# Turning a tile of activations with VectorE block turns and block transfers in place of TensorE transposes

## The chip, the cores and the metric

The kernel runs on one core of a Trainium2 chip. The metric is the device time of one execution in microseconds (us). The engines are TensorE (PE in the profile; its weight loads are PEld), VectorE (DVE), ScalarE (ACT), GpSimd (POOL) and SyncE (SP, which here only issues DMA transfers). SBUF is the on-chip memory of 128 partitions, PSUM the eight banks that TensorE writes its products to, and HBM the memory outside.

## The reference

The input `x` is 2048 rows of 512. Each row is normalised, and two branches are added to it: an attention-like retrieval from a fixed memory, and a dense layer with int8 weights.

```python
xn = _layernorm(x, axis=-1)
# retrieval; only every 4th head of q is used, and each is repeated 4 times
q = (xn @ Wq.T + bq).reshape(b, s, 32, 128)
q_sel = (elu(q) + 1.0)[:, :, ::4, :]                      # 8 heads of 128
num = jnp.einsum('bshd,hde->bshe', q_sel, M)
den = jnp.einsum('bshd,hd->bsh', q_sel, z)[..., None] + 1e-6
out_heads = jnp.repeat(num / den, 4, axis=2)
attn = out_heads.reshape(b, s, 4096) @ Wo.T
# dense
ffn = jnp.einsum('bsd,df->bsf', xn, w.astype(jnp.float32) * w_scale) + b
return x + attn + ffn
```

The kernel multiplies M and Wo (summed over its 4 repeats) once into `P`, so that per row there are three products: q (512 to 1024), dense (512 to 512), and attn (1024 to 512), whose left side is `a` = (elu(q) + 1) / den.

## The kernel before

The rows are cut into 16 tiles (`t`) of 128. Every product is done in three passes of 32-bit matmuls, high times high, high times low and low times high, for which each operand is split into a part rounded to `float32r` (`_hi`, by ScalarE) and a rest (`_lo`, by VectorE). Weights, `WqT`, `wd` and `P`, are split once; `xT` and `aT`, the transposed activations, once a tile.

What each engine does, and in which order, is written out by hand. A list of about 40 lines a engine covers the loading and splitting of weights, the products q, dense of tiles 0 to 6 and the eight products that make `P` (`product_P`). From tile 7 (`LEAD`) a loop over `t` runs, and after tile 15 a tail, since the attention product stands 7 tiles behind q. In one turn `t` of the loop:

- TensorE does `product_q(t)` in two halves, `product_dense(t)`, the spreading of a mean (`spread_mean`), `product_attn(t - 7)` and `transpose_a(t - 5)`; in the tail only `product_attn` and `transpose_a`.
- VectorE adds the bias (`add_bias`), makes `s` = elu(q) + 1 (`make_s`) in a ring of 7 buffers, sums `s` times z over each head (`denominator`), splits `aT_lo` (`split_aT_lo`) and adds the finished products to `x` (`add_dense`, `add_attn`).
- ScalarE does the exponential, divides `s` by its head's denominator in place (`make_a`, eight activations a tile), and copies `aT` to `aT_hi` (`copy_aT_hi`).
- GpSimd multiplies `s` by z (`times_z`), adds `b`, centres `xT`.
- SP issues the loads of `x` and `xT` and the stores of the finished tiles.

`transpose_a` is 8 matmuls of 128x128 against a unit matrix `ident`. They turn `a` of a tile, rows on partitions, into `aT`, columns on partitions, in the two PSUM banks `aT_ps`; `copy_aT_hi` and `split_aT_lo` read them there. The buffers `aT_hi` and `aT_lo` have two places, so a copy for tile t waits until `product_attn(t - 2)` is done (`attn_filled`).

Of the kernel before, what the change touches and what calls it, by code (L numbers as in the profile page):

```python
# [15 lines left out]
DEN_EPS = 1e-6  # L16


def retrieval_and_dense(nc, x_d, xT_d, WqT_d, bq_d, WoT_d, MT_d, z_d, w_d, wscale_d, b_d, out_d):
# [4 lines left out]
    G, D = z_d.shape  # L24
# [7 lines left out]
    SRING = 7  # L32
    XRING = 4
    HRING = 4
    BEHIND = 4
    assert P == D and HID == 512 and HALF == 512 and R == 4 and T == 16 and G == 8 and K == 4

    with ExitStack() as ctx:
# [35 lines left out]
        den = sb("den", [P, G])  # L74
        den_e = sb("den_e", [P, G])
        rden = sb("rden", [P, 2, G])
        warm_b = sb("warm_b", [P, HID], BF16)

        warm_r = P_hi[:, 0, :]
        w_i8 = w_words[:].bitcast(I8)  # L80
        WqT_raw = sbuf_s[:, 0:K, :]
        wd_raw = sbuf_s[:, K:K + 2, :].rearrange("p r (a n) -> p (r a) n", n=HID)
        ebuf = e_and_sz[:, 0, :]
        szbuf = e_and_sz[:, 1, :]
        w_f32 = e_and_sz[:].rearrange("p r (a n) -> p (r a) n", n=HID)
# [8 lines left out]
        def q_bank(t, h):  # L94
            return ([q_ps, attn_ps, aT_ps][t % 3] if t < LEAD else q_ps)[h]
# [13 lines left out]
        consts_set = sem("consts_set")  # L109
        stats_set = sem("stats_set")  # L110
# [27 lines left out]
        den_e_ready = sem("den_e_ready")  # L138
# [5 lines left out]
        aT_filled = sem("aT_filled")  # L144
# [15 lines left out]
        def _(sp):  # L160
# [24 lines left out]
            sp.dma_start(w_words[:], w_d).then_inc(w_in, 16)  # L185
# [9 lines left out]
            sp.dma_start(z_b[:].rearrange("p (g d) -> p g d", g=G),  # L195
                         z_d.unsqueeze(0).to_broadcast([P, G, D])).then_inc(z_in, 16)
            sp.dma_start(b_b[:], b_d.unsqueeze(0).to_broadcast([P, HID])).then_inc(b_in, 16)
            for t in range(5, T):
                if t >= FIRST_LENT:
                    sp.wait_ge(P_filled, t - FIRST_LENT + 1)  # L200
                load_x(t)
                load_xT(t)
                if t >= 10:
                    sp.wait_ge(attn_added, t - 9)
                    sp.dma_start(out_d[t - 10], x[:, t - 10, :]).then_inc(stored, 16)
            for t in range(T - 10, T - 1):
                sp.wait_ge(attn_added, t + 1)
                sp.dma_start(out_d[t], x[:, t, :]).then_inc(stored, 16)
# [7 lines left out]
        def _(pool):  # L216
# [31 lines left out]
            def times_z(t, h):  # L248
                if t == 0 and h == 0:
                    pool.wait_ge(z_in, 16)  # L250
                if t == 0:
                    pool.wait_ge(wd_by_pool, 1)
# [3 lines left out]
                nc.gpsimd.tensor_tensor(szbuf[:, halves(h)], sbuf_s[:, t % SRING, halves(h)],  # L256
                                        z_b[:, halves(h)], ALU.mult).then_inc(sz_ready, 1)
# [20 lines left out]
            scale_w()  # L278
            rstd_of(3)
# [20 lines left out]
            center(7)  # L300
            add_b(0)
# [9 lines left out]
            for t in range(T - BEHIND, T):  # L311
                times_z(t, 0)
                times_z(t, 1)
                add_b(t - BEHIND + 2)
            for t in range(T - 2, T):
                add_b(t)

        @block.scalar
        def _(act):
# [58 lines left out]
            def copy_aT_hi(t):  # L378
                for h in range(2):
                    act.wait_ge(aT_filled, 2 * t + h + 1)  # L380
                    if t >= 2:
                        act.wait_ge(attn_filled, t - 1)
                    nc.scalar.activation(aT_hi[:, t % 2, h * GH:(h + 1) * GH, :].rearrange("p g r -> p (g r)"),  # L383
# [514 lines left out]
```

## Time and profile before

| | |
|---|---|
| median of 3 runs | 260.02 us (259.87 to 264.77) |
| the profiled execution | 260.27 us |
| its span, from the first to the last instruction | 258.5 us |
| TensorE busy | 249.9 us, 97% of the span |
| VectorE, ScalarE, GpSimd busy | 156.2, 121.2, 103.2 us |
| bytes moved by DMA | 26.42 MB, mean 102 GB/s |
| TensorE's granted clock | 1.0 in all 40 slices |

The profile comes from one execution, whose own time is 1.8 us above its span and 0.25 us above the median of the runs. Busy time is added up per engine and engines run beside each other, so a share near 100% names the engine to look at first, and the chain of waits tells whether it sets the end. Ends of matmuls are modelled: they overlap, and the pitch from start to start is what one costs.

### The profile page before, as it was taken

The numbers are of one execution on the slowest core, as the hardware profiler recorded it, in microseconds if no ns is written. First come the engines' busy times: TensorE is split into PE (matmuls) and PEld (weight loads), VectorE is DVE, ScalarE is ACT, GpSimd is POOL, SyncE is SP. The second block draws the span as 40 slices with busy tenths as digits, with TensorE's granted clock in tenths as the row PEclk, the third lists the DMA queues.
The fourth block names the chain that finished last, engine by engine and source line by source line (L and its number), as shares of the span: only waits on it lengthen the run. The fifth ranks groups of instructions, "written<-read, shape, count | busy, mean of one in ns | idle before, by whom it ended". The sixth has DMA issues, their size and how long they took to land.

```text
span 258.5 us, 3387 instructions
## 1 busy us (share of the span) xinstructions
PE 249.9 (97%) x1156; PEld 201.2 (78%) x1156; DVE 156.2 (60%) x262; ACT 121.2 (47%) x276; POOL 103.2 (40%) x96
## 2 busy tenths in 40 slices
PE   6899899899998999999999999999999999999996
PEld 4477687687766888888888888888888888888885
DVE  4849996898677846457483746557463445555321
ACT  3653625657457554444345553544345345555100
POOL 2594745580303670705235070714305055563000
PEclk9999999999999999999999999999999999999999
DMA  7999999995400003030302103010101001111111
GB/s 247 414 411 406 345 228 218 209 217 153 146 16 4 0 13 109 0 124 1 122 1 66 58 0 122 3 41 0 41 3 41 1 1 43 41 41 43 49 49 64
DMA packets 9808, 26.42 MB, mean 102 GB/s; under 512 B 1088, under 2 KB 1344, under 8 KB 8640
## 3 DMA queue, kind: packets, MB, share of 16 engines
q1 hardware_dynamic: 8640, 19.40, 20.2%
q0 software_dynamic: 864, 6.29, 11.8%
q10 hardware_dynamic: 288, 0.52, 0.6%
q8 instruction: 9, 0.15, 0.2%
q14 instruction: 7, 0.06, 0.1%
HBM read 22.02 MB, written 4.19 MB: 101 GB/s over the span
## 4 chain that ended last, share of the span: by engine, by line
PE 84%; DVE 9%; ACT 2%; issue 2%; DMA 1%; DVEq 0%
PE attn_ps L679 11%; PE attn_ps L677 11%; PE attn_ps L678 11%; PE q_ps L677 8%; PE q_ps L679 8%; PE q_ps L678 8%; PE aT_ps L752 5%; PE dense_ps L677 5%; PE dense_ps L678 5%; PE dense_ps L679 5%; PE attn_ps L740 2%; DMA x<-in_x 1%; DVE stats L462 1%; DVE wd_lo L517 1%; DVE q_ps L531 1%
## 5 line engine op out<-in xcount | busy, mean ns | idle before, releaser
L256 POOL TENSOR_TENSOR e_and_sz<-s,z_b 128x512 f32<-128x512 f32 x32 | 41.7, 1330 | 31.4 <-DVE den L543 31.4
L375 ACT ACTIVATE s<-s,rden 128x128 f32<-128x128 f32 x128 | 39.2, 389 | 31.0 <-DVE rden L550 31.0
L677 PE MATMUL attn_ps<-P_hi,aT_hi 128*128 128x512 f32 (+1 forms) x128 | 50.2, 393 | 0.0
L679 PE MATMUL attn_ps<-P_hi,aT_lo 128*128 128x512 f32 (+1 forms) x128 | 49.2, 385 | 0.0
L678 PE MATMUL attn_ps<-P_lo,aT_hi 128*128 128x512 f32 (+1 forms) x128 | 49.0, 382 | 0.0
L570 DVE TENSOR_TENSOR x<-attn_ps,x 128x512 f32<-128x512 f32 x15 | 10.4, 691 | 46.4 <-PE attn_ps L679 46.4
L677 PE MATMUL q_ps<-WqT_hi,xT_hi 128*128 128x512 f32 x88 | 36.0, 409 | 0.6 <-DVE s L538 0.6
L679 PE MATMUL q_ps<-WqT_hi,xT_lo 128*128 128x512 f32 x88 | 34.4, 391 | 0.0
L678 PE MATMUL q_ps<-WqT_lo,xT_hi 128*128 128x512 f32 x88 | 34.3, 390 | 0.0
L219 POOL TENSOR_TENSOR rstd<-vareps,neg_half 128x1 f32<-128x1 f32 x16 | 10.6, 665 | 55.7 <-DVE vareps L470 55.7
L225 POOL TENSOR_TENSOR xT<-xT,mean_b 128x512 f32<-128x512 f32 x14 | 19.6, 1403 | 32.5 <-ACT mean_b L324 32.5
L531 DVE SCALAR_TENSOR_TENSOR q_ps<-q_ps,rstd,bq_b 128x512 f32<-128x512 f32 x24 | 18.1, 758 | 21.5 <-PE q_ps L679 21.5
L362 ACT ACTIVATE e_and_sz<-q_ps 128x512 f32<-128x512 f32 x24 | 14.3, 596 | 33.9 <-DVE q_ps L531 33.9
L679 PEld LDWEIGHTS attn_ps<-P_hi,aT_lo 128*128 128x128 f32 x128 | 24.1, 188 | 4.9
L677 PEld LDWEIGHTS attn_ps<-P_hi,aT_hi 128*128 128x128 f32 x128 | 24.1, 188 | 4.9
L678 PEld LDWEIGHTS attn_ps<-P_lo,aT_hi 128*128 128x128 f32 x128 | 24.1, 188 | 4.4
L677 PE MATMUL dense_ps<-wd_hi,xT_hi 128*128 128x512 f32 x64 | 25.6, 400 | 1.2 <-DVE x L554 1.2
L383 ACT ACTIVATE aT_hi<-aT_ps 128x512 fp32r<-128x512 f32 x32 | 17.4, 595 | 17.0 <-PE aT_ps L752 17.0
L679 PE MATMUL dense_ps<-wd_hi,xT_lo 128*128 128x512 f32 x64 | 24.9, 390 | 0.0
L678 PE MATMUL dense_ps<-wd_lo,xT_hi 128*128 128x512 f32 x64 | 24.9, 390 | 0.0
L563 DVE TENSOR_TENSOR aT_lo<-aT_ps,aT_hi 128x512 fp32r<-128x512 f32 x32 | 20.6, 685 | 5.2 <-ACT aT_hi L383 5.2
L364 ACT ACTIVATE e_and_sz<-e_and_sz 128x512 f32<-128x512 f32 x32 | 20.2, 632 | 1.0
(93 smaller groups left out, 407.9 us busy)
## 6 DMA issues: line engine op xcount, KB each, us to landing
x<-in_WoT POOLq DMA_DIRECT2D x6, 1024.0 KB, 9.6
x<-in_x SPq DMA_DIRECT2D x16, 256.0 KB, 3.7
xT<-in_xT SPq DMA_DIRECT2D x16, 256.0 KB, 4.1
out<-x SPq DMA_DIRECT2D x15, 256.0 KB, 2.0
x<-in_WoT SPq DMA_DIRECT2D x2, 1024.0 KB, 14.6
s<-in_WqT SPq DMA_DIRECT2D x3, 512.0 KB, 7.0
s<-in_w_scale SPq DMA_DIRECT2D x1, 1024.0 KB, 10.1
s<-in_WqT ACTq DMA_DIRECT2D x2, 256.0 KB, 4.2
```

The source lines that it names most:

```text
L225: nc.gpsimd.tensor_tensor(xT[:, t % XRING, :, :], xT[:, t % XRING, :, :], mean_b[:, t % 2, :].unsqueeze(1).to_broadcast([P, K, P]), ALU.su ...
L256: nc.gpsimd.tensor_tensor(szbuf[:, halves(h)], sbuf_s[:, t % SRING, halves(h)], z_b[:, halves(h)], ALU.mult).then_inc(sz_ready, 1)
L362: nc.scalar.activation(e, q_bank(t, h)[:], ACT.Relu, scale=-1.0).then_inc(qneg_ready, 1)
L364: nc.scalar.activation(e, e, ACT.Exp, scale=-1.0).then_inc(exp_ready, 1)
L375: last = nc.scalar.activation(a_g, a_g, ACT.Copy, scale=rden[:, t % 2, g:g + 1])
L383: nc.scalar.activation(aT_hi[:, t % 2, h * GH:(h + 1) * GH, :].rearrange("p g r -> p (g r)"), aT_ps[h][:], ACT.Copy).then_inc(aT_hi_ready, 1)
L531: nc.vector.scalar_tensor_tensor(q_bank(t, h)[:], q_bank(t, h)[:], rstd[:, t:t + 1], bq_b[:, halves(h)], ALU.mult, ALU.add).then_inc(q_bia ...
L563: nc.vector.tensor_tensor(aT_lo[:, t % 2, gs, :].rearrange("p g r -> p (g r)"), aT_ps[h][:], aT_hi[:, t % 2, gs, :].rearrange("p g r -> p ...
L677: nc.tensor.matmul(out, x_hi, w_hi, start=start, stop=False)
L678: nc.tensor.matmul(out, x_hi, w_lo, start=False, stop=False)
L679: return nc.tensor.matmul(out, x_lo, w_hi, start=False, stop=stop)
L752: last = nc.tensor.transpose(aT_ps[h][:, i * P:(i + 1) * P], sbuf_s[:, t % SRING, g * D:(g + 1) * D], ident[:])
```

## The change

The transposes leave TensorE. A 128x128 transpose is made of 32x32 blocks that are turned inside a quarter of the partitions, and a move of each block from its quarter of the partitions to another.

- `turn_blocks(t)`: one VectorE instruction turns all 32x32 blocks of `s` of a tile (128x1024) in place.
- `spread_blocks(t)`: SP issues 16 transfers a tile, SBUF to SBUF, each of 32 partitions by 256 elements (1 KB runs), from partition quarter i and column quarter j to partition quarter j and place i of `aT`. Tiles take two places in turn: a new buffer `aT` and the buffer of `MT`, which is free once `P` is made.
- For that q, bq, z and `s` are laid out by quarters of heads (first columns 0 to 31 of all 8 heads, then 32 to 63, and so on). `make_a` and `times_z` now read and write rows of 32 elements (`by_quarter`), and `copy_aT_hi` and `split_aT_lo` read SBUF in place of PSUM (`by_head`, `in_groups`).
- The epsilon of the denominator becomes a 129th column of each head's products, which the sum takes along; the instruction that added it goes.
- The two PSUM banks of `aT` become two more banks of q, so that q of a tile has to wait for `s` of the tile before the last one only.
- `make_a` and the sums run one tile earlier (`BEHIND` 3 for 4), the ring of `s` has 6 places for 7. SP's list is written anew around the 16 transfers. The matmuls that keep TensorE at work at the start read a 128x128 bf16 tile, 8 and 6 of them for 7 and 5, and two early loads change places.

```diff
-    SRING = 7
+    SRING = 6
-    BEHIND = 4
+    BEHIND = 3
...
-        q_ps = [bank("q0_ps"), bank("q1_ps")]
-        aT_ps = [bank("aT0_ps"), bank("aT1_ps")]
+        q_ps = [bank(f"q{i}_ps") for i in range(4)]
...
+        def by_quarter(v):
+            return v.rearrange("p (j g c) -> p j g c", g=G, c=D // 4)
+        def aT_place(t):
+            return [aT[:], MT[:].rearrange("p g d -> p (g d)").rearrange("p (i e) -> p i e", i=4)][t % 2]
+        def by_head(t, gs):
+            return aT_place(t).rearrange("p i (g r) -> p g i r", g=G)[:, gs]
...
+            def spread_blocks(t):
+                sp.wait_ge(a_turned, t + 1)
+                if t == 1:
+                    sp.wait_ge(P_filled, G)
+                elif t >= 2:
+                    sp.wait_ge(aT_lo_ready, 2 * t - 2)
+                for i in range(4):
+                    for j in range(4):
+                        sp.dma_start(aT_place(t)[j * 32:(j + 1) * 32, i, :],
+                                     sbuf_s[i * 32:(i + 1) * 32, t % SRING, j * E // 4:(j + 1) * E // 4]
+                                     ).then_inc(aT_in[t % 2], 16)
...
+            for t in range(LEAD, T):
+                if t + 4 < T:
+                    sp.wait_ge(P_filled, t + 4 - FIRST_LENT + 1)
+                    load_x(t + 4)
+                    load_xT(t + 4)
+                spread_blocks(t - BEHIND - 1)
+                if t - LEAD >= 1:
+                    store(t - LEAD - 1)
+            for t in range(T - BEHIND - 1, T):
+                spread_blocks(t)
+                store(t - BEHIND - 1)
...
             def copy_aT_hi(t):
+                act.wait_ge(aT_in[t % 2], aT_landed(t))
+                if t >= 2:
+                    act.wait_ge(attn_filled, t - 1)
...
-                nc.vector.reduce_sum(den[:], szbuf.rearrange("p (g d) -> p g d", g=G), AX.X
-                                     ).then_inc(den_ready, 1)
+                nc.vector.reduce_sum(den[:, t % 2, :], sz_eps, AX.X).then_inc(den_ready, 1)
                 dve.wait_ge(den_ready, t + 1)
-                nc.vector.tensor_scalar_add(den_e[:], den[:], DEN_EPS).then_inc(den_e_ready, 1)
...
+            def turn_blocks(t):
+                dve.wait_ge(a_ready, t + 1)
+                nc.vector.transpose(sbuf_s[:, t % SRING, :], sbuf_s[:, t % SRING, :]).then_inc(a_turned, 1)
...
-            def transpose_a(t):
-                pe.wait_ge(a_ready, t + 1)
...
-                transpose_a(t - LEAD + 2)
```

On TensorE, at the end of a turn of the loop, the order before is this; L679 is the last pass of `product_attn`, L752 `transpose_a`, and L677 the first pass of the next `product_q`.

```order
637 L677 MATMUL attn_ps<-P_hi,aT_hi 128x512
638 L678 MATMUL attn_ps<-P_lo,aT_hi 128x512
639 L679 MATMUL attn_ps<-P_hi,aT_lo 128x512
640 L752 MATMUL aT_ps<-ident,s 128x128 x8
641 L677 MATMUL q_ps<-WqT_hi,xT_hi 128x512
642 L678 MATMUL q_ps<-WqT_lo,xT_hi 128x512
```

The same place now has no row between the last pass of `product_attn` and `product_q`.

On SP, from the last loads to the end of the program, the order before:

```order
46 L162 DMA x<-in_x 128x512 [waits P_filled]
47 L167 DMA xT<-in_xT 128x512 [waits xT_lo_ready]
48 L205 DMA out<-x 128x512 [waits attn_added]
49 L208 DMA out<-x 128x512 [waits attn_added] x9
50 L212 DMA out<-x 128x256 [waits attn_added] x2
51 L38 UNCONDITIONAL_BRANCH [waits stored]
```

And after the change, from the blocks of tile 12 to the end; L200 is `spread_blocks`, L206 `store`.

```order
75 L200 DMA aT<-s 32x256 [waits aT_lo_ready,a_turned]
76 L200 DMA aT<-s 32x256 x15
77 L206 DMA out<-x 128x512 [waits attn_added]
78 L200 DMA MT<-s 32x256 [waits aT_lo_ready,a_turned]
79 L200 DMA MT<-s 32x256 x15
80 L206 DMA out<-x 128x512 [waits attn_added]
81 L200 DMA aT<-s 32x256 [waits aT_lo_ready,a_turned]
82 L200 DMA aT<-s 32x256 x15
83 L206 DMA out<-x 128x512 [waits attn_added]
84 L200 DMA MT<-s 32x256 [waits aT_lo_ready,a_turned]
85 L200 DMA MT<-s 32x256 x15
86 L206 DMA out<-x 128x512 [waits attn_added] x4
```

Sixteen transfers of tiles 12, 13, 14 and 15 each now stand in SP's queue in the tail, with a store of an earlier tile between them; before there were only stores.

On VectorE, from the last `add_dense` of the loop into the tail, the order before:

```order
207 L554 SCALAR_TENSOR_TENSOR x<-dense_ps,rstd,x 128x512
208 L543 TENSOR_REDUCE den<-e_and_sz 128x8
209 L546 TENSOR_SCALAR den_e<-den 128x8
210 L550 RECIPROCAL rden<-den_e 128x8
211 L570 TENSOR_TENSOR x<-attn_ps,x 128x512
212 L563 TENSOR_TENSOR aT_lo<-aT_ps,aT_hi 128x512 x2
```

And after the change:

```order
209 L599 SCALAR_TENSOR_TENSOR x<-dense_ps,rstd,x 128x512
210 L591 TENSOR_REDUCE den<-e_and_sz 128x8
211 L595 RECIPROCAL rden<-den 128x8
212 L591 TENSOR_REDUCE den<-e_and_sz 128x8
213 L595 RECIPROCAL rden<-den 128x8
214 L619 TENSOR_TENSOR x<-attn_ps,x 128x512
215 L612 TENSOR_TENSOR aT_lo<-aT,aT_hi 128x512 x2
216 L604 STREAM_TRANSPOSE s<-s 128x1024
```

Two sums, of tiles 12 and 13, stand there in a row now, and the turn of tile 12 stands behind `add_attn(8)` and `split_aT_lo(10)`.

## Rows read from the trace of the kernel before

**Rows 1.** The page: busy time by engine (us, share, instructions), and the chain by engine.

```profile
PE 249.9 (97%) x1156; PEld 201.2 (78%) x1156; DVE 156.2 (60%) x262; ACT 121.2 (47%) x276; POOL 103.2 (40%) x96
...
PE 84%; DVE 9%; ACT 2%; issue 2%; DMA 1%; DVEq 0%
```

**Rows 2.** Busy time in four stretches: end of P, loop, tail, last tile.

```profile
core 0: us, PE busy (x) PEld busy (x) DVE busy (x) ACT busy (x) POOL busy (x), PEclk, DMA share, GB/s
74.88:81.27 6.39, 5.70 (x27) 3.27 (x26) 5.46 (x10) 4.91 (x13) 0.33 (x1) 1.00 0.00 0
81.27:211.89 130.62, 130.62 (x612) 108.21 (x611) 73.96 (x128) 60.85 (x144) 51.78 (x46) 1.00 0.11 37
211.89:249.50 37.61, 37.61 (x191) 31.68 (x190) 17.88 (x30) 16.34 (x44) 14.36 (x12) 1.00 0.11 43
```

**Rows 3.** The chain in order of time: start us, us, what; transposes alone.

```profile
109.73 0.87 PE aT_ps L752 x8
...
124.38 0.87 PE aT_ps L752 x8
...
237.45 0.87 PE aT_ps L752 x8
...
243.82 0.87 PE aT_ps L752 x8
```

**Rows 4.** Timeline of PE at the end of `P`, before tile 7.

```profile
79.19 1.10 PE L740 MATMUL attn_ps<-x,MT 128*128 128x512 f32 x2 [0.69 <-DVE P_lo L522]
80.13 1.04 PE L752 MATMUL aT_ps<-ident,s 128*128 128x128 f32 x8
81.00 0.27 PE L687 MATMUL mean_ps<-ident,meanvar 128*128 128x128 f32 x1
```

**Rows 5.** Timeline of DVE there.

```profile
80.49 0.18 DVE L466 BATCH_NORM_AGGREGATE meanvar<-stats 128x2 f32<-128x6 f32 x1
```

**Rows 6.** Timeline of SP's queue: loads issued one behind another, and lone stores.

```profile
1.65 0.42 SPq L162 DMA_DIRECT2D x<-in_x  x1
2.12 0.43 SPq L170 DMA_DIRECT2D s<-in_WqT  x1
...
15.60 2.34 SPq L162 DMA_DIRECT2D x<-in_x  x1
...
250.90 0.33 SPq L208 DMA_DIRECT2D out<-x  x1
```

**Rows 7.** DMA queue of SP and ACT (packets, MB, share of 16 engines), and stores to landing.

```profile
q1 hardware_dynamic: 8640, 19.40, 20.2%
...
out<-x SPq DMA_DIRECT2D x15, 256.0 KB, 2.0
```

**Rows 8.** Timeline of DVE in the last turn of the loop.

```profile
203.93 0.76 DVE L531 SCALAR_TENSOR_TENSOR q_ps<-q_ps,rstd,bq_b 128x512 f32<-128x512 f32 x1 [1.88 <-PE q_ps L679]
...
206.01 0.69 DVE L538 SCALAR_TENSOR_TENSOR s<-q_ps,e_and_sz 128x512 f32<-128x512 f32 x1 [0.74 <-ACT e_and_sz L364]
...
207.31 1.21 DVE L543 TENSOR_REDUCE den<-e_and_sz 128x8 f32<-128x1024 f32 x1
```

**Rows 9.** Timeline of POOL and of PE (first pass of `product_attn(8)`) there.

```profile
208.60 2.54 POOL L256 TENSOR_TENSOR e_and_sz<-s,z_b 128x512 f32<-128x512 f32 x2 [10.71 <-DVE den L543]
...
206.44 0.39 PE L677 MATMUL attn_ps<-P_hi,aT_hi 128*128 128x512 f32 x1
```

**Rows 10.** Timeline of DVE and ACT behind `product_attn(8)`.

```profile
212.09 0.69 DVE L570 TENSOR_TENSOR x<-attn_ps,x 128x512 f32<-128x512 f32 x1 [2.90 <-PE attn_ps L679]
213.16 1.29 DVE L563 TENSOR_TENSOR aT_lo<-aT_ps,aT_hi 128x512 fp32r<-128x512 f32 x2 [0.38 <-ACT aT_hi L383]
...
212.53 1.09 ACT L383 ACTIVATE aT_hi<-aT_ps 128x512 fp32r<-128x512 f32 x2 [0.85 <-PE aT_ps L752]
```

**Rows 11.** Timeline of DVE and POOL at 18 to 21 us.

```profile
18.70 2.53 DVE L500 TENSOR_TENSOR xT_lo<-xT,xT_hi 128x512 fp32r<-128x512 f32 x1 [3.77 <-ACT xT_hi L339]
...
18.29 2.39 POOL L237 TENSOR_TENSOR s<-e_and_sz,s 128x1024 f32<-128x1024 f32 x1 [0.43 <-ACT e_and_sz L349]
```

More of the change, by code:

```diff
@@ L94, in q_bank @@
         def q_bank(t, h):
-            return ([q_ps, attn_ps, aT_ps][t % 3] if t < LEAD else q_ps)[h]
+            if t < LEAD and t % 3 == 1:
+                return attn_ps[h]
+            return q_ps[2 * (t % 3 == 2 if t < LEAD else t % 2) + h]
         def last_attn_ps(c):
@@ L143, in retrieval_and_dense @@
         dense_added = sem("dense_added")
-        aT_filled = sem("aT_filled")
+        a_turned = sem("a_turned")
+        aT_in = [sem(f"aT_in{i}") for i in range(2)]
         aT_hi_ready = sem("aT_hi_ready")
@@ L194, in _ @@
             load_xT(4)
-            sp.dma_start(z_b[:].rearrange("p (g d) -> p g d", g=G),
-                         z_d.unsqueeze(0).to_broadcast([P, G, D])).then_inc(z_in, 16)
+            sp.dma_start(z_b[:], z_d.unsqueeze(0).to_broadcast([P, E])).then_inc(z_in, 16)
             sp.dma_start(b_b[:], b_d.unsqueeze(0).to_broadcast([P, HID])).then_inc(b_in, 16)
-            for t in range(5, T):
-                if t >= FIRST_LENT:
-                    sp.wait_ge(P_filled, t - FIRST_LENT + 1)
+            for t in range(5, FIRST_LENT):
                 load_x(t)
                 load_xT(t)
[L203 to L208, printed above, removed]
+            spread_blocks(0)
+            for t in range(FIRST_LENT, LEAD + 4):
+                sp.wait_ge(P_filled, t - FIRST_LENT + 1)
+                load_x(t)
+                load_xT(t)
+            spread_blocks(1)
+            spread_blocks(2)
+            for t in range(LEAD, T):
[9 more added lines that the diff above has]
+                store(t - BEHIND - 1)
+            for t in range(T - BEHIND - 1, T - 1):
+                store(t)
             for c in range(2):
@@ L300, in _ @@
             center(7)
+            times_z(3, 0)
+            times_z(3, 1)
             add_b(0)
@@ L313, in _ @@
                 times_z(t, 1)
-                add_b(t - BEHIND + 2)
-            for t in range(T - 2, T):
+                add_b(t - 3)
+            for t in range(T - 3, T):
                 add_b(t)
@@ L441, in _ @@
             copy_mean(8)
+            make_a(3)
             for t in range(LEAD, T):
-                copy_aT_hi(t - LEAD + 1)
                 exp_of(t, 0)
@@ L452, in _ @@
                 copy_aT_hi(t)
-                if t + 2 < T:
-                    make_a(t + 2)
+                if t + BEHIND < T:
+                    make_a(t + BEHIND)
         @block.vector
@@ L633, in _ @@
             split_P_lo(1)
+            turn_blocks(1)
             add_dense(5)
@@ L648, in _ @@
             split_P_lo(7)
+            turn_blocks(2)
             for t in range(LEAD, T):
-                split_aT_lo(t - LEAD + 1)
                 add_bias(t, 0)
@@ L658, in _ @@
                 make_s(t, 1)
+                split_aT_lo(t - LEAD + 1)
                 add_dense(t)
                 denominator(t - BEHIND)
+                if t == T - 1:
+                    denominator(T - BEHIND)
                 add_attn(t - LEAD)
@@ L741, in product_P @@
                                  ).then_inc(P_filled, 1)
-            def transpose_a(t):
-                pe.wait_ge(a_ready, t + 1)
-                for h in range(2):
-                    if t == 0:
-                        pe.wait_ge(s_ready, 11 + h)
-                    else:
-                        pe.wait_ge(aT_lo_ready, 2 * t - 1 + h)
-                    for i in range(GH):
-                        g = h * GH + i
-                        last = nc.tensor.transpose(aT_ps[h][:, i * P:(i + 1) * P],
-                                                   sbuf_s[:, t % SRING, g * D:(g + 1) * D], ident[:])
-                    last.then_inc(aT_filled, 1)
             def product_attn(t):
@@ L765, in product_attn, with keep_busy @@
                 last.then_inc(attn_filled, 1)
[L767 to L771 removed]
+            def keep_busy(n):
+                for i in range(n):
+                    nc.tensor.matmul(dense_ps[:], warm[:], warm[:].unsqueeze(1).to_broadcast([P, 4, P]), start=True, stop=True)
+            pe.wait_ge(warm_set, 1)
+            keep_busy(8)
             pe.wait_ge(consts_set, 3)
             spread_mean(0)
[L774 to L775 removed]
+            keep_busy(6)
             hi_hi(0, 0, 0)
```

98 lines of the change are left out of this document (48 added, 50 removed).

## The prediction

> **What bounds the kernel now.** I read the page's busy times first, then the chain of waits, then the busy time by stretch, and last the timelines of single engines. TensorE is busy 97% of the span, and 84% of the chain that ended last is its own work [rows 1]. The stretches show where that is strictly so: from tile 7 to the end of the loop it is busy 130.62 of 130.62 us, and in the tail 37.61 of 37.61 [rows 2]. VectorE, ScalarE and GpSimd stand at 74, 61 and 52 us in the loop's 131. So whatever leaves TensorE's list there comes off the end, as long as nobody else is late. The transposes of one tile cost 0.87 us on the chain, whichever tile; they come every 14.65 us in the loop (109.73 to 124.38) and every 6.37 us in the tail (237.45 to 243.82) [rows 3]. Without them a turn of the loop would be 13.78 us. A `product_attn` is 5.45 us (from 206.44 to 211.89, where the third stretch of the windows begins) [rows 2, 9], which is also what a tile of the tail would cost.
>
> **Part 1, the transposes go.** Sixteen tiles are turned: nine in the loop (tiles 2 to 10), five in the tail (11 to 15), two before tile 7. In loop and tail nothing else stands between TensorE's products, so 14 x 0.87 = 12.2 us go. The two before tile 7 save nothing: there the products of `P` wait for their own split (0.69 us before the last one at 79.19), a wait that takes in what the first transpose gives up, and `spread_mean(8)` needs a mean that VectorE has at 80.49 + 0.18 = 80.67, against TensorE's 81.00 now [rows 4, 5]. That leaves 0.3 us, and the new turn and sum on VectorE in that stage (about 2.6 us, partly in its waits) may cost as much or a little more: I take 0, with -0.5 to +0.9 as bounds of the gain. The span without new waits is 258.5 - 12.2 = 246.3 us.
>
> **Part 2, VectorE.** It gets one turn of 128x1024 a tile and loses one small addition. No row shows a turn; the nearest is the sum over 128x1024, 1.21 us [rows 8], which I take; the upper bound is GpSimd's 2.39 us for the same size [rows 11]. `split_aT_lo` now has two SBUF operands. Such an instruction took 2.53 us at 18.70 while GpSimd's ran from 18.29 for 2.39, so it waited for it to end [rows 11]; the split from PSUM took 1.29 for two [rows 10]. That is up to 1.3 us a half more. The loop's cover holds: 73.96 us busy in nine turns is 8.2 a turn, and 8.2 + 1.2 + 2.6 = 12.0 is below 13.78. Cost in the loop 0; with the cover gone each us above it would cost nine. The Trainium skill (VectorE: DVE Perf Modes, section "The three transpose paths", and its rules for authors) speaks against this trade: it gives 390 ns for a 128x128 bf16 transpose on TensorE and 311 on VectorE, in blocks only, and says to use TensorE where PSUM will do. By its figure eight of them are 2.5 us of VectorE, which the loop would still cover; the rows price TensorE's eight at 0.87 us, less than a third of its figure.
>
> **Part 3, ScalarE and GpSimd.** `make_a` and `times_z` get rows of 32 elements for 128 or 512; sizes stay. I take the same durations, and twice as the bound. ScalarE has 60.85 us busy in nine turns, 6.8 of 13.78, GpSimd 5.8 [rows 2]; doubling these parts still fits. Cost 0. The new q banks loosen a wait that TensorE does not have in this stretch: 0. The start keeps its order but for two loads: 0, give or take 0.3.
>
> **Part 4, SP's queue.** Sixteen transfers a tile are issued one behind another by one engine. SP's loads at the start are issued every 0.47 us (1.65, 2.12), 0.42 to 0.43 us long; a lone store after a wait takes 0.33 [rows 6]. All these have 128 rows; a transfer of 32 rows is in no row. If the price is one of the instruction and not of its rows, it is 0.47 us; if rows count, it goes towards the 0.33 of the lone one plus the gap of 0.04, or 0.37. I take 0.47, since 4 KB rows (2.12) are issued as fast as 2 KB rows (1.65), and a lone instruction may have been made ready during its wait. In the loop 16 x 0.47 + 3 x 0.47 = 8.9 us a turn fit in 13.78, and each tile's blocks have two turns of time: cost 0. In the tail a tile lasts 5.45 us and SP needs 16 x 0.47 + 0.47 = 8.0. There it decides.
>
> **The tail, step by step.** Let T be the end of `product_attn(8)`, 211.89 in the trace before. What is worked out here is relative to it, so the gain of part 1 shifts all alike. VectorE's last turn: `add_bias` at 203.93, 0.66 to its next instruction, turn(11) 1.2, two `make_s` 1.3, the two splits of tile 9 1.3, `add_dense` 0.6 (make_s and it lie 1.30 apart from 206.01 to 207.31), sum and reciprocal of tile 12 1.5: 210.5 [rows 8]. The sum of tile 13 needs two `times_z`, 2.54 us [rows 9], begun when the first sum is over: 212.9, its own 1.4 to 214.3. Then `add_attn(8)` 0.7, the splits of tile 10 1.3, the turn of tile 12 1.2 [rows 10]: 217.5, or T + 5.6. GpSimd works on tile 14 just then, so I add 0.6 for one wait of a split: T + 6.2, bounds T + 5.6 and, with a turn of 2.4 and two full waits, T + 9. Now SP issues tiles 12 to 15: 64 transfers and 3 stores between them, 67 x 0.47 = 31.5. The last lands 2.0 us after its issue begins [rows 7], which adds 1.5, and then half a copy to `aT_hi` and half a split, 1.3 [rows 10], stand before `product_attn(15)`: T + 6.2 + 31.5 + 1.5 + 1.3 = T + 40.5. TensorE could begin it at T + 6 x 5.45 = T + 32.7. It is 7.8 us late, shared as waits before tiles 13 (about 2.6), 14 and 15. With pitch p the lateness is 7.8 - 66 x (0.47 - p).
>
> **Sum.** 246.3 + 7.8 = 254.1 us span; the profiled execution lies 1.8 above its span, and the median 0.25 below that: 255.6 us.
>
> **The rivals.**
>
> *The small transfers are issued faster.* At 0.37 us the tail is late by 7.8 - 6.6 = 1.2 us: 249.0 us. With all bounds in its favour it is 247.5, at 0.42 it is 252.3. For it: the lone store, 0.33 us, and a quarter of the rows. Against it: no issue in a series, whatever its bytes, was below 0.42. The Trainium skill (DMA: Bandwidth & Descriptors, section "Issuing engines are not separate DMA queues") is on this side: it calls the issuing time usually small beside the transfer. The rows of SP show 0.47 us an issue beside 2.0 us to landing for 256 KB, and a block has 32 KB.
>
> *The transfers themselves hold the queue back.* When the queue was full in the first 20 us, one issue took 2.34 us [rows 6]. A block is 32 packets of data and, by the 144 packets of a 128-row load (8640 for 60 transfers), 16 more: 3 an engine. Packets took 20.2% of 16 x 258.5 us for 8640, 97 ns each [rows 7], so a block would need 0.29 us, under the pitch. If a packet within SBUF took 0.2 us, the pitch were 0.6 and the tail 8.6 us later: 264.2. This is the case on the other side. From 0.54 on it is no gain at all, from 0.62 slower by over 2%, and above 0.77 the loop's 13.78 us are exceeded too.
>
> *The strided operands cost double, or the turn.* VectorE's tail then starts SP two to three us later, and a few waits enter the loop: 257 to 260 us.
>
> *The change does not do what it says:* were aT not ready early in the loop (tile 1 waits for all of `P`), TensorE would wait at tile 8 or 9. SP has from 80 us on 7.5 us an issue of a tile, and `product_attn(1)` comes 22 us later, so I give this no time of its own.
>
> **How the numbers follow.** The forecast, a pitch between 0.43 and 0.50 (253 to 257.5), 0.45. Faster issue, 247 to 253, 0.37. Held back by transfers, 258 to 272, 0.11. Strides, 0.07. The predicted time is 255.6 us. The range of 8 in 10 leaves out the lowest of the fast case and the upper part of the held-back one: 247.5 to 261. Within 2% (254.8 to 265.2) is about what a measurement of this kernel can tell from no change; the forecast lies just inside. Faster by over 2%: all of the fast case and some 0.13 of the forecast, 0.50. Slower by over 2%: 0.06. Between: 0.44.
>
> **What would show it.** Part 1: no transposes on PE, turns of the loop 13.8 us apart, PE busy all of it. Part 4: SP's issues of 32x256 every 0.47 us in runs of 16, no gap between runs from tile 12 on; PE idle before `product_attn(13)`, (14) and (15) for about 2.6 us each, released by VectorE's `aT_lo`, that by ScalarE's `aT_hi`, that by DMA. If PE is idle in the loop, a cover of part 2 or 3 has failed; if the tail has no idle PE, the pitch was lower. I would be most wrong if the transfers queue up.

## The result

The changed kernel takes 270.86 us (median of 4, 269.67 to 271.33) where the kernel before takes 260.0: the ratio is 1.041, with a 95% interval from 1.037 to 1.046. It is slower by 4%; I had forecast 255.6 us and given a slower kernel 6 in 100. Runs of the kernel before spread from 259.8 to 264.9 us, for a reason that no run here shows, so every experiment below has its ratio to runs of that kernel on the same chip, and two experiments are compared by their own times and by their profiled spans.

The page of the changed kernel, first the busy times, then the granted clock in 40 slices, SP's queue, the chain by engine and by line, and the costliest group:

```profile
PE 245.0 (91%) x1030; PEld 191.5 (71%) x1030; DVE 176.4 (65%) x261; ACT 119.8 (44%) x276; POOL 106.0 (39%) x97
...
PEclk9999999999999999999999999999999999868968
...
q1 hardware_dynamic: 20928, 27.81, 31.8%
...
PE 61%; SPq 18%; DVE 10%; issue 4%; ACT 3%; DMA 2%; DVEq 0%
SPq L200 18%; PE q_ps L734 9%; PE q_ps L736 9%; PE q_ps L735 8%; PE attn_ps L734 7%; PE attn_ps L736 7%; PE attn_ps L735 7%; PE dense_ps L734 4%; PE dense_ps L736 4%; PE dense_ps L735 4%; PE attn_ps L797 2%; DVE stats L510 1%; DMA x<-in_x 1%; DVE wd_lo L565 1%; DVE s L586 1%
...
L734 PE MATMUL attn_ps<-P_hi,aT_hi 128*128 128x512 f32 (+1 forms) x128 | 53.4, 417 | 14.8 <-DVE aT_lo L612 14.8
```

TensorE's share of the chain fell from 84% [rows 1] to 61%, and one line of SP's queue, the issue of the sixteen transfers, holds 18% of the span. TensorE waits 14.8 us for `aT_lo` in all. Where that is, the busy times by stretch say (loop, tail in four pieces, the product of tile 13 alone, and the first 6 us of the last product):

```profile
core 0: us, PE busy (x) PEld busy (x) DVE busy (x) ACT busy (x) POOL busy (x), PEclk, DMA share, GB/s
...
100.00:206.00 106.00, 106.00 (x466) 86.51 (x465) 75.09 (x110) 52.65 (x128) 42.27 (x38) 1.00 0.29 86
...
220.00:230.00 10.00, 7.23 (x31) 5.56 (x30) 3.03 (x4) 3.49 (x10) 1.35 (x2) 1.00 0.26 75
230.00:240.00 10.00, 5.03 (x13) 3.67 (x12) 3.02 (x4) 1.15 (x2) 0.00 (x0) 0.67 0.26 75
240.00:250.00 10.00, 7.22 (x25) 5.54 (x24) 1.90 (x3) 1.15 (x2) 0.00 (x0) 0.84 0.24 71
250.00:260.00 10.00, 5.72 (x24) 4.61 (x24) 1.90 (x3) 1.15 (x2) 0.00 (x0) 0.84 0.34 112
...
234.00:240.00 6.00, 4.39 (x10) 3.48 (x11) 3.02 (x4) 1.15 (x2) 0.00 (x0) 0.50 0.30 89
...
258.00:264.00 6.00, 6.00 (x28) 6.00 (x29) 1.56 (x3) 0.00 (x0) 0.00 (x0) 0.50 0.20 74
```

The loop is full, as it was before [rows 2]: the cover of VectorE, ScalarE and GpSimd held. The tail, full before, is not: TensorE has 7.23, 5.03, 7.22 and 5.72 us of work in four times 10 us, and its granted clock falls, to half (1.2 GHz) while it works on tile 13 and again in the last product. VectorE, ScalarE and GpSimd idle too, so none of them is the bound. SP's queue is what never rests:

```profile
201.31 10.01 SPq L200 DMA_DIRECT2D MT<-s  x16
211.35 0.58 SPq L206 DMA_DIRECT2D out<-x  x1
212.03 10.02 SPq L200 DMA_DIRECT2D aT<-s  x16
222.09 0.58 SPq L206 DMA_DIRECT2D out<-x  x1
222.77 10.03 SPq L200 DMA_DIRECT2D MT<-s  x16
...
233.52 10.01 SPq L200 DMA_DIRECT2D aT<-s  x16
...
244.25 11.02 SPq L200 DMA_DIRECT2D MT<-s  x16
```

Sixteen issues take 10.0 us, and a tile 10.74 (212.03 to 222.77), so an issue costs 0.633 us with its gap, where I had taken 0.47. A tile of the tail needs 5.60 us of TensorE (5.45 before the change). The chain in order of time shows the same issues one by one, and then the steps by which the last tile reaches TensorE:

```profile
247.34 1.60 SPq L200
...
254.05 0.59 SPq L200
254.69 1.87 DMA MT<-s
256.58 0.64 ACT aT_hi L431
257.24 0.70 DVE aT_lo L612
257.99 0.58 PE attn_ps L734
```

The last transfer lands 1.87 us after its issue began, and issues follow one another every 0.63 us (254.05, 254.69): the transfers themselves are quick, the issues are what queues. By the shares of the queue in the two profile pages (31.8% of 16 x 269.4 us, less 20.2% of 16 x 258.5) the 12288 packets of the blocks took some 44 ns each, an estimate, so 48 of them on 16 engines take 0.13 us. TensorE's waits in the tail, in the brackets of its timeline, are before the products of tiles 12 to 15:

```profile
224.81 0.47 PE L734 MATMUL attn_ps<-P_hi,aT_hi 128*128 128x512 f32 x1 [2.77 <-DVE aT_lo L612]
235.61 0.77 PE L734 MATMUL attn_ps<-P_hi,aT_hi 128*128 128x512 f32 x1 [4.97 <-DVE aT_lo L612]
246.35 0.47 PE L734 MATMUL attn_ps<-P_hi,aT_hi 128*128 128x512 f32 x1 [2.78 <-DVE aT_lo L612]
257.99 0.58 PE L734 MATMUL attn_ps<-P_hi,aT_hi 128*128 128x256 f32 x1 [4.28 <-DVE aT_lo L612]
```

The matmul at 235.61 takes 0.77 us and the one at 246.35 takes 0.47: the first runs at the lower clock, as do the matmuls behind it up to 240 us. The releaser named is VectorE, but VectorE is idle there; followed back, it waits for ScalarE's copy, that for the landing, and that for the issue. This is the wait that the prediction describes, only larger, and it begins one tile earlier, before tile 12.

### The profile page after: what moved, and what is told of

It is laid out like the page before. It is cut to its first block, busy times and chain, and to the rows that moved or that the text cites. A ratio compares the mean times of both kernels' runs of the same rounds, so it can differ in the third digit from the quotient of the medians.

```text
span 269.4 us, 3377 instructions
## 1 busy us (share of the span) xinstructions
PE 245.0 (91%) x1030; PEld 191.5 (71%) x1030; DVE 176.4 (65%) x261; ACT 119.8 (44%) x276; POOL 106.0 (39%) x97
## 2 busy tenths in 40 slices
DMA packets 22097, 34.83 MB, mean 129 GB/s; under 512 B 5184, under 2 KB 13632, under 8 KB 20928
## 3 DMA queue, kind: packets, MB, share of 16 engines
q1 hardware_dynamic: 20928, 27.81, 31.8%
q0 software_dynamic: 864, 6.29, 11.4%
## 4 chain that ended last, share of the span: by engine, by line
PE 61%; SPq 18%; DVE 10%; issue 4%; ACT 3%; DMA 2%; DVEq 0%
SPq L200 18%; PE q_ps L734 9%; PE q_ps L736 9%; PE q_ps L735 8%; PE attn_ps L734 7%; PE attn_ps L736 7%; PE attn_ps L735 7%; PE dense_ps L734 4%; PE dense_ps L736 4%; PE dense_ps L735 4%; PE attn_ps L797 2%; DVE stats L510 1%; DMA x<-in_x 1%; DVE wd_lo L565 1%; DVE s L586 1%
## 5 line engine op out<-in xcount | busy, mean ns | idle before, releaser
L734 PE MATMUL attn_ps<-P_hi,aT_hi 128*128 128x512 f32 (+1 forms) x128 | 53.4, 417 | 14.8 <-DVE aT_lo L612 14.8
L298 POOL TENSOR_TENSOR e_and_sz<-s,z_b 128x512 f32<-128x512 f32 x32 | 42.8, 1367 | 43.1 <-DVE den L591 43.0
L735 PE MATMUL attn_ps<-P_lo,aT_hi 128*128 128x512 f32 (+1 forms) x128 | 52.2, 408 | 0.0
L734 PE MATMUL q_ps<-WqT_hi,xT_hi 128*128 128x512 f32 x104 | 41.8, 402 | 0.9 <-DVE s L586 0.6
L736 PE MATMUL q_ps<-WqT_hi,xT_lo 128*128 128x512 f32 x104 | 40.6, 390 | 0.0
L735 PE MATMUL q_ps<-WqT_lo,xT_hi 128*128 128x512 f32 x104 | 40.5, 390 | 0.0
L612 DVE TENSOR_TENSOR aT_lo<-MT,aT_hi 128x512 fp32r<-128x512 f32 x16 | 15.3, 993 | 17.6 <-ACT aT_hi L431 17.6
L586 DVE SCALAR_TENSOR_TENSOR s<-q_ps,e_and_sz 128x512 f32<-128x512 f32 x28 | 18.8, 676 | 7.9 <-DMA MT<-s 4.0
L734 PEld LDWEIGHTS q_ps<-WqT_hi,xT_hi 128*128 128x128 f32 x104 | 19.5, 188 | 6.0 <-issue 1.2
L612 DVE TENSOR_TENSOR aT_lo<-aT,aT_hi 128x512 fp32r<-128x512 f32 x16 | 14.8, 966 | 12.2 <-ACT aT_hi L431 12.2
L735 PEld LDWEIGHTS q_ps<-WqT_lo,xT_hi 128*128 128x128 f32 x104 | 19.5, 188 | 4.4 <-issue 0.5
```

The lines of the kernel that those rows point to most:

```text
L298: nc.gpsimd.tensor_tensor(sz_eps[:, :, h * D // 2:(h + 1) * D // 2].rearrange("p g (j c) -> p j g c", j=2), by_quarter(sbuf_s[:, t % SRING ...
L586: nc.vector.scalar_tensor_tensor(sbuf_s[:, t % SRING, halves(h)], q_bank(t, h)[:], 0.0, ebuf[:, halves(h)], ALU.max, ALU.add).then_inc(s_r ...
L612: nc.vector.tensor_tensor(in_groups(aT_lo[:, t % 2, gs, :]), by_head(t, gs), in_groups(aT_hi[:, t % 2, gs, :]).bitcast(F32), ALU.subtract) ...
L734: nc.tensor.matmul(out, x_hi, w_hi, start=start, stop=False)
L735: nc.tensor.matmul(out, x_hi, w_lo, start=False, stop=False)
L736: return nc.tensor.matmul(out, x_lo, w_hi, start=False, stop=stop)
```

## The experiments

Two questions stood: is it the number of issues that costs, and what sets the price of one? And what makes up the rest, since 66 issues at 0.633 us explain some 11 of the 15 us by which the forecast was missed?

**Four issues for sixteen.** A transfer takes 32 rows with four runs each and writes all 128 partitions; the rows and columns of `a` come in another order, and the matrix `M` is laid out to fit.

```diff
-                    for j in range(4):
-                        sp.dma_start(aT_place(t)[j * 32:(j + 1) * 32, i, :],
-                                     sbuf_s[i * 32:(i + 1) * 32, t % SRING, j * E // 4:(j + 1) * E // 4]
+                    sp.dma_start(aT_place(t)[:, i, :],
+                                 sbuf_s[i * 32:(i + 1) * 32, t % SRING, :].rearrange("r (j c) -> r j c", j=4)
...
```

> The changed kernel with 4 transfers a tile in place of 16: each takes one quarter of the partitions (32 rows of 4 runs of 1 KB) and lays its runs on all 128 partitions in the order row, column quarter; M's columns are laid out to match, so the bytes moved and the result stay the same. Theory, a transfer has a price per instruction on SP of about 0.63 us whatever its rows: SP needs 4 x 0.63 + 0.6 = 3.1 us a tile, less than the 5.6 of a tile of the tail, so no product of the tail waits; the end of the eighth attention product at 205.0 us + 6 x 5.6 + 8.5 gives a span of 247 us and a time near 249 us. Rival, the price goes by runs or bytes: 4 issues take as long as 16 did, 10 us a tile, and the time stays near 270 us.

Measured: 248.81 us (248.55 to 249.08), ratio 0.947 (0.942 to 0.952). SP's queue and the tail by stretch:

```profile
211.74 2.50 SPq L199 DMA_DIRECT2D aT<-s  x4
214.28 0.59 SPq L205 DMA_DIRECT2D out<-x  x1
217.64 2.50 SPq L199 DMA_DIRECT2D MT<-s  x4
...
204.00:238.00 34.00, 34.00 (x148) 27.36 (x147) 24.64 (x28) 15.95 (x43) 16.58 (x12) 1.00 0.45 125
```

Each issue now moves four times the bytes and costs the same 0.63 us; SP waits between tiles, TensorE is full. The bytes are the same as with sixteen, 27.8 MB on this queue. The packets are fewer, 17856 for 20928, but took more of the engines' time together (36.1% of 16 x 247.1 us for 31.8% of 16 x 269.4), so the loss lay in the count of issues. With **eight** issues of 64 partitions a tile:

> The changed kernel with 8 transfers a tile, each of 32 rows of 2 runs laid on 64 partitions, M's columns laid out to match; bytes and result are the same. Theory, an issue within SBUF costs 0.60 us of SP (0.63 from start to start) whatever it carries: SP needs 8 x 0.63 + 0.63 = 5.7 us a tile in the tail, where TensorE needs 5.6, so the tail waits for a few tenths at most and the time is within 1 us of the kernel with 4, 248.8 us. Rival, halving the transfers halves the loss: about 259 us.

Measured: 249.13 us (248.44 to 249.66), ratio 0.954 (0.947 to 0.961), no wait of TensorE in the tail. Eight at 0.63 and a store are 5.7 us, level with the 5.6 us between two tiles. So up to eight issues the count costs nothing that the time shows; between eight and sixteen no run stands.

**What an issue costs.** Behind the end of the kernel before, seven batches of transfers are issued by SP, each batch waited for. They differ in rows, bytes, runs and in where the data lies.

```diff
+            for i in range(16):
+                sp.dma_start(sbuf_s[i % 4 * 32:(i % 4 + 1) * 32, 0, i // 4 * 256:(i // 4 + 1) * 256],
+                             sbuf_s[i // 4 * 32:(i // 4 + 1) * 32, 1, i % 4 * 256:(i % 4 + 1) * 256]
+                             ).then_inc(priced[0], 16)
+            sp.wait_ge(priced[0], 256)
...
+                sp.dma_start(sbuf_s[i % 4 * 32:(i % 4 + 1) * 32, 0, i // 4 * 256:(i // 4 + 1) * 256],
+                             x_d[i][i // 4 * 32:(i // 4 + 1) * 32, 0:256]).then_inc(priced[2], 16)
```

> The kernel before the change, and behind its last store seven batches on SP's queue, each waited for before the next: 16 transfers within SBUF of 32x256 between quarters, 16 within SBUF of 128x256, 16 from HBM of 32x256, 12 from HBM of 128x512, 16 within SBUF from 32 rows of 4 runs to 128x256, 16 within SBUF of 128x16 (64-byte runs), and 16 to HBM of 32x256. The issue durations of each are read from the trace. Theory, per instruction: the first, third and last batch come out at one duration and all lie within 0.42 to 0.63 us. Rival A, transfers within SBUF are dearer to issue than those that touch HBM: first, second, fifth and sixth near 0.6, the others near 0.43. Rival B, a slice of 32 partitions is dearer: first, third and last near 0.6, the others near 0.43.

SP's queue, in this order: within SBUF 32 rows of 1 KB; 128 rows of 1 KB; HBM to SBUF 32 rows of 1 KB; 128 rows of 2 KB (twelve of them); within SBUF 32 rows of four runs; 128 rows of 64 bytes; SBUF to HBM 32 rows of 1 KB:

```profile
259.27 10.11 SPq L217 DMA_DIRECT2D s<-s  x16
270.64 10.46 SPq L220 DMA_DIRECT2D s<-s  x16
282.60 7.31 SPq L223 DMA_DIRECT2D s<-in_x  x16
291.18 5.75 SPq L226 DMA_DIRECT2D s<-in_x  x12
302.18 10.40 SPq L229 DMA_DIRECT2D s<-s  x16
314.61 10.17 SPq L232 DMA_DIRECT2D s<-s  x16
325.99 7.29 SPq L235 DMA_DIRECT2D scratch<-s  x16
```

Divided by their counts: 0.63, 0.65, 0.46, 0.48, 0.65, 0.64, 0.46 us. Neither a quarter of the rows nor a sixteenth of the bytes changes it by more than 0.02 us; source and destination do. With HBM on one side an issue costs 0.46 to 0.48 us, with SBUF on both 0.63 to 0.65. A page of the Trainium skill (DMA: Bandwidth & Descriptors, section "Issuing engines are not separate DMA queues") calls the issuing time usually small beside the transfer. Here it is a third of the 1.8 us to landing, and since sixteen transfers overlap and their issues don't, it is the bound.

These are prices in a series of one kind. Part of the price stands with the neighbour: in the loop of the changed kernel a load from HBM takes 0.58 us directly behind the transfers within SBUF, and the load behind it 0.44.

```profile
112.36 0.58 SPq L178 DMA_DIRECT2D x<-in_x  x1
112.98 0.44 SPq L183 DMA_DIRECT2D xT<-in_xT  x1
```

The stores between two tiles of the tail take 0.58 us for the same reason, as far as these rows tell; what SP waits for there no run shows.

**Two queues.** In the tail (tiles 12 to 15) half of the sixteen are issued by ScalarE.

```diff
+                if t + 2 >= 12 and t + 2 < T:
+                    act.wait_ge(a_turned, t + 3)
+                    act.wait_ge(aT_lo_ready, 2 * (t + 2) - 2)
+                    for i in range(2, 4):
+                        for j in range(4):
+                            act.dma_start(aT_place(t + 2)[j * 32:(j + 1) * 32, i, :],
...
```

> The changed kernel, 16 transfers a tile, but those of tiles 12 to 15 issued half by SP and half by ScalarE's queue, there behind the copy of the tile two before and the scaling of the tile one after. Theory, each issuing engine pays for its own issues and the generators do not hinder each other: SP needs 5.7 us a tile, ScalarE 8 x 0.63 + 1.2 + 2.5 = 8.7, and the last tile lands some 13 us earlier than at 256.6: a span near 256 us and a time near 258. Rival, the issues of both share one generator: 10 us a tile again, and the time stays at 268 to 271 us.

Measured: 262.06 us (260.9 to 263.59), ratio 1.002 (0.997 to 1.007). From the timelines of ScalarE and of SP's queue:

```profile
238.38 5.30 ACTq L508 DMA_DIRECT2D MT<-s  x8
243.78 1.15 ACT L431 ACTIVATE aT_hi<-aT 128x512 fp32r<-128x512 f32 x2 [7.39 <-issue]
...
238.37 4.96 SPq L200 DMA_DIRECT2D MT<-s  x8
```

SP and ScalarE issue eight each at the same time, at 0.62 and 0.66 us an issue. So the price is paid per issuing engine, not in something that they share: some 9 us come back (262.06 for 270.86). That it is 4 us more than I expected (3.4 in the span, 259.4 for 256) is mostly my own edit: ScalarE's issues for tile 15 stand ahead of its copy for tile 14, which so begins at 243.78, and the product of tile 14 at 245.28, behind a wait of TensorE of 2.70 us.

**The clock.** Matmuls on unused data fill TensorE's waits in the tail (10, 20, 20 and 20 of them behind tiles 11 to 14).

```diff
+                if t >= T - LEAD + 2:
+                    keep_busy(10 if t == T - LEAD + 2 else 20)
```

> The changed kernel with 10, 20, 20 and 20 further bf16 matmuls of 128x512 on TensorE, of zeros into a PSUM bank that nobody reads any more, behind the attention products of tiles 11 to 14, where TensorE waits. Theory, the fall of the granted clock in the tail costs only what the last product takes longer, 8.7 us against about 5.9 at full clock: the granted clock stays at 1.0 for the last product, and the time falls by 2 to 3 us, to about 268 us. Rival, the waits alone make the loss: no difference, or up to 2 us more where the added matmuls overrun the gap.

Measured: 268.28 us (267.98 to 269.27), ratio 1.022 (1.016 to 1.028); its slowest run is below the fastest of the changed kernel (269.67), and the medians are 2.6 us apart. The granted clock stays at full where it was 0.67 and 0.84, and only the last product has no issue behind which to hide: it starts at 258.17 (257.99 in the changed kernel) and the span ends 8.6 us later where it was 11.4:

```profile
230.00:240.00 10.00, 8.21 (x37) 4.71 (x37) 3.02 (x4) 1.15 (x2) 0.00 (x0) 1.00 0.25 72
...
258.17 0.39 PE L734 MATMUL attn_ps<-P_hi,aT_hi 128*128 128x256 f32 x1 [0.46 <-DVE aT_lo L612]
```

So the clock costs 2.8 us of the span, all of it in the last product, a loss on top of the waits that go before it.

**The distance of two passes.** In the changed kernel the 24 passes of a product with `a` lie further apart than those of the other products. The first pass of `product_attn(8)` and the first of `product_attn(9)`, 24 places later, in the changed kernel:

```profile
199.48 0.39 PE L734 MATMUL attn_ps<-P_hi,aT_hi 128*128 128x512 f32 x1
...
205.08 0.40 PE L734 MATMUL attn_ps<-P_hi,aT_hi 128*128 128x512 f32 x1
```

That is 5.60 us for 24 places, 0.2333 each, where the other products have 0.227. The change put a buffer of 8224 bytes (`e_and_sz`, with the column for epsilon) ahead of `aT_hi`, which so lies 32 bytes off. A first try put 32 unused bytes behind it, so that `aT_hi` lies 64 bytes off:

> The changed kernel with 8 unused columns (32 bytes) behind the buffer of the exponentials and products with z, so that the buffers behind it, aT_hi and aT_lo first, start at a multiple of 64 bytes as before the change. Theory, the attention passes are issued every 0.233 us for 0.227 before, and their weight loads take 204 ns for 188, because aT_hi and aT_lo lie 32 bytes off: weight loads back to 188 ns, passes every 0.227 us, the eighth attention product ends 1.3 us earlier, and since SP's issues set the tail, the time falls by about 1.3 us only. Rival, the slower passes come from the block transfers that write SBUF beside them: weight loads stay at 204 ns, no difference.

Measured: 269.56 us (267.91 to 270.89), ratio 1.025 (1.019 to 1.031), and the passes still 0.2333 us apart. The profiled span is 269.3 us, as the changed kernel's 269.4, so I don't count the median as a gain. The expectation's 204 ns for a weight load was the mean of the whole trace of the changed kernel, the tail at half clock with it: from 100 to 200 us its loads take 188 ns, as before the change. The second try, on the kernel with four issues, allocates `e_and_sz` last, and `aT_hi` lies at a multiple of 2048 bytes:

```diff
-        e_and_sz = sb("e_and_sz", [P, E + G * (D + 1)])
...
         warm = sb("warm", [P, P], BF16)
+        e_and_sz = sb("e_and_sz", [P, E + G * (D + 1)])
```

> The kernel with 4 transfers a tile, and the buffer of the exponentials and products with z placed behind all other buffers in SBUF, so that aT_hi and aT_lo start at a multiple of 2048 bytes again, as before the change (in the changed kernel they lie 32 bytes off, and 64 in the kernel of the second experiment). Theory, the attention passes, 0.2333 us apart in every changed kernel so far at full clock against 0.227 before, are slower because of that address: they come back to 0.227, 24 x 0.006 x 16 = 2.3 us off the span of 247.1: 244.8, and a time near 246.5. Rival, something else of the change makes them slower: 0.2333 and 248.8 us.

Measured: 246.8 us (246.47 to 247.69), ratio 0.945 (0.939 to 0.952); the profiled span 245.1 us for 247.1. The same two passes:

```profile
198.47 0.39 PE L733 MATMUL attn_ps<-P_hi,aT_hi 128*128 128x512 f32 x1
...
203.91 0.39 PE L733 MATMUL attn_ps<-P_hi,aT_hi 128*128 128x512 f32 x1
```

5.44 us, 0.2267 each. Then the address alone, in the kernel before the change, which has nothing else of it (`aT_hi`, `aT_lo` and the buffers behind them move; `P_hi` and `P_lo` lie ahead and stay):

```diff
+        unused = sb("unused", [P, 8])
         aT_hi = sb("aT_hi", [P, 2, G, P], F32R)
```

> The kernel before the change, with 32 unused bytes a partition ahead of aT_hi and of what lies behind it, and nothing else. In the changed kernels a pass of the products with a took 0.2333 us where aT_hi lay off a large power of two and 0.227 where it lay on one. Theory (the address of the operand sets it, without any other part of the change): the 24 passes of each of the 16 products take 0.2333 us instead of 0.227, 384 x 0.0064 = 2.4 us more, ratio 1.009. Rival (the slower pass belongs to the new layout of a or to traffic within SBUF): 0.227 as before, ratio 1.000.

Measured: 264.42 us (261.85 to 266.69), ratio 1.006 (1.0005 to 1.012), a small difference. The trace is plainer: passes with `aT_hi` 0.233 us apart in loop and tail (0.228 in the kernel before), those of the other products unchanged at 0.226 to 0.228, the span 260.4 us for 258.5. With 384 passes 0.005 us further apart 1.9 us are due and 1.9 are there; my 2.4 were reckoned from 0.227. Then 256 and 128 unused bytes, with one run each:

> As the run with 32 unused bytes, with 256 bytes instead: one look at the distance of two passes. If it is the multiple of 64 or 256 bytes that matters, a pass takes 0.227 us; if it is a larger one (in the changed kernel a shift to a multiple of 64 bytes left 0.2333), 0.2333 us.

> The kernel before the change with 128 unused bytes a partition ahead of aT_hi: one look at the distance of two passes. 32 bytes gave 0.233 us and 256 bytes 0.228. No theory says which side 128 is on; this bounds where the slower pass begins.

Passes 0.228 us apart at 256 bytes, 0.2325 at 128. So shifts of 32 and 128 bytes slow them (and 64 in the changed kernel), 256 does not. `aT_hi` and `aT_lo` are the operands that are loaded as weights, yet their loads take 188 ns in the kernel before and in the shifted ones alike; by what means the address counts no run shows.

**The sixteen issues with the buffer moved.** Does the slower pass explain the tail?

> The changed kernel with its sixteen transfers a tile, and only the buffer e_and_sz allocated last, so that aT_hi lies on a multiple of 2048 bytes. Theory: its passes go back to 0.227 us, which brings the end of the ninth product of the loop forward by about 0.9 us; the tail behind it is set by SP's 0.63 us an issue and not by TensorE, so the four microseconds and more of waits stay, and the half clock with them: 271 less 1, about 270. Rival (the slower passes were what cost the tail): it would fall by the 2.4 us of all products and the waits with it, to 266 or below.

Measured: 269.19 us (268.09 to 270.21), ratio 1.032 (1.027 to 1.037), span 267.4 us. The waits are there still (3.41, 3.74, 2.32 and 5.96 us), and so is the half clock:

```profile
256.95 0.58 PE L734 MATMUL attn_ps<-P_hi,aT_hi 128*128 128x256 f32 x1 [5.96 <-DVE aT_lo L612]
```

Of the 2.0 us less span, the last product starts 1.04 earlier (256.95 for 257.99); this is the part of the address, as the theory has it. The other 0.96 lies in the last product: the granted clock is back to full at 260.7 us here and only at 264.1 in the changed kernel, and why no run shows. The address is a part of its own, not the cause.

**The sum in the lead.** In the kernel with four issues and the moved buffer, one reduction of VectorE is put behind the splits of `P`.

```diff
+            denominator(3)
...
-            denominator(3)
```

> The kernel of the run with four transfers a tile and aT_hi in its aligned place (246.8 us), with one thing moved: the sum of the exponentials of head 3 (VectorE's reduction of 1.22 us, at 72.9 us) is taken later, behind the split of head 7, so that VectorE reaches the splits of P before the products of P sooner. In that run TensorE waits 0.82, 0.70 and 0.43 us (together 1.95) at 76.9, 78.7 and 80.2 us; before the change it waited 0.69 us once. Theory (the second block turn put ahead of these splits made VectorE late for them, and what TensorE waits there is lost for good): the first wait goes and the others shrink, about 1 us less, 245.8. Rival (the waits are only passed on to the next product of P, since VectorE works without a pause up to there): 246.8, within 0.3.

Measured: 247.06 us (246.59 to 247.71), ratio 0.944 (0.937 to 0.951): no change. The first wait went from 0.82 to 0.65 us, the others stayed. The rival is right; VectorE is busy up to there, and what is last is its whole work, not this sum.

## Why the prediction was wrong

**Part 1 held, on both sides.** With four issues and the moved buffer, `product_attn(8)` begins at 198.47 us where it began at 206.44 [rows 9]: 7.97 us earlier. Loop turns are 13.75 us in that kernel, so the transposes of a tile gave back 0.90 us rather than 0.87. The lead, which I took at 0 with a bound of 0.9, gave 0.7: in the changed kernel the mean of tile 8 is spread at 80.27 us where it was 81.00 [rows 4], with three waits of 0.82, 0.71 and 0.43 us ahead.

```profile
76.94 1.10 PE L797 MATMUL attn_ps<-x,MT 128*128 128x512 f32 x2 [0.82 <-DVE P_lo L570]
78.74 1.10 PE L797 MATMUL attn_ps<-x,MT 128*128 128x512 f32 x2 [0.71 <-DVE P_lo L570]
80.27 0.32 PE L744 MATMUL mean_ps<-ident,meanvar 128*128 128x128 f32 x1 [0.43 <-DVE meanvar L514]
```

That kernel's span is 245.1 us, where part 1 had 246.3 without new waits. **Parts 2 and 3 held.** From VectorE's timeline in the tail:

```profile
207.64 2.90 DVE L612 TENSOR_TENSOR aT_lo<-aT,aT_hi 128x512 fp32r<-128x512 f32 x2
210.46 1.23 DVE L604 STREAM_TRANSPOSE s<-s 128x1024 f32<-128x1024 f32 x1
```

The turn is 1.23 us (taken: 1.2). By the figure of the Trainium skill (VectorE: DVE Perf Modes, section "The three transpose paths"), 311 ns for a 128x128 block in bf16, eight are 2.5 us, an estimate that the trace does not bear out for this one instruction in fp32. Two splits beside GpSimd are 2.90 us for 1.28 alone, within the 2.6 us more that I allowed. `make_a` takes 389 ns before and after, `times_z` 1367 for 1330.

**Part 4 failed, in one number.** The step was "If the price is one of the instruction and not of its rows, it is 0.47 us". It is one of the instruction; rows and bytes don't count, as I argued, though the transfer ahead of it does. But the rows I took it from are loads from HBM, and a transfer within SBUF is another instruction: 0.633 us. The case on the other side, with its pitch of 0.6, came true in its size by another mechanism, and I had given it 0.11 because I looked for it in the packets, which were not the limit: with 0.633 the prediction's own formula gives 266.4 us.

The formula of the tail was right, and the rows split up what is left. Eight of the loop's nine transposes stand ahead of the end of `product_attn(8)` (that of tile 10 comes behind it, at 211.89), so by the forecast this end lies at 211.89 - 8 x 0.87 = 204.93 us, and the last product should begin 40.5 us later, at 245.43. It began at 257.99, 12.56 later:

- The end of `product_attn(8)`, 205.08 for 204.93, gives 0.15. The slower passes of nine products cost 1.17 (it is 203.91 with the buffer moved), and the lead and the cheaper transposes take back 1.02.
- From there to SP's first issue of tile 12 (212.03) it is 6.95 us for 6.2: 0.75. VectorE has turned tile 12 at 211.69; SP is busy with tile 11 and a store until 211.93. So it is SP's own queue that comes last here too, which the prediction left out.
- From that issue to SP's last (254.69) it is 42.66 us for 31.0: 11.66. Sixty-six pitches make 10.7 of it, and one issue of 1.60 us the rest.
- Landing and copies take 3.30 us for 3.3.

Behind the last product's start 11.41 us were left for 8.67 (254.1 - 245.43): 2.74, which is the half clock. 12.56 and 2.74 are the 15.3 us between 254.1 and 269.4.

Two sums on the side were off as well. The waits were to begin before tile 13, and at 0.633 us they begin before tile 12. The pitch above which the loop's turn is exceeded is 13.78 / 19 = 0.73 us and not 0.77, since a turn has 19 issues.

**What was not foreseen at all** are the clock (2.8 us) and the address (1.0 to 1.2 us in the changed kernel, where SP sets the tail; 2.0 us of span with four issues, where TensorE does). The first hangs on the waits; the second is a cost of the column for epsilon, whose 32 bytes shift what lies behind them.

Left open: what makes an issue within SBUF dearer, and why one to or from HBM takes 0.58 us right behind it and 0.42 to 0.44 behind its own kind; the one issue of 1.60 us at 247.34 (with the buffer moved the sixteen of tile 15 also take 11.02 us for 10.01); and by what means the address counts.

## What to carry to other kernels

A transfer has a price at the engine that issues it, and it has to be taken from a row with the same source and destination memory; the count of issues between two deadlines, times that price, is compared with the time between them before anything else. If it doesn't fit, fewer transfers with more runs each carry the same bytes, or a second engine issues some, but not ahead of work that the tail waits for. And where a change adds a small buffer, look at what it shifts.

## What the runs showed of the hardware

- In a series of its own kind an issue on SP costs 0.46 to 0.48 us with HBM on one side (32 to 256 KB) and 0.63 to 0.65 us within SBUF (8 to 128 KB), for 32 or 128 rows; a load right behind transfers within SBUF took 0.58 us for 0.44. SP and ScalarE issued eight each side by side, at 0.62 and 0.66 us.
- Waits of TensorE of 2.77 and 4.97 us in the tail were followed by a granted clock of half (1.2 GHz), and one of 4.28 us was again; with matmuls in the waits it stayed at 2.4 GHz.
- Matmul passes lie 0.233 us apart for 0.227 or 0.228 when the buffer of the operand that is loaded as weights is shifted by 32, 64 or 128 bytes, and not when by 256. The loads take 188 ns either way.
- A turn of 32x32 blocks over 128x1024 floats takes VectorE 1.23 us; TensorE's eight transposes of the same data cost 0.87 to 0.90 us of its stream.
